# Audio attention: averages in four 32-column tiles of one bank, half of the keys turned by TensorE

## The reference

```python
a = _layer_norm(audio_kv, ln_gamma, ln_beta)              # 8 batches x 1500 tokens x 256
Q = (hidden_states @ Wq.T)...                             # 8 batches x 56 queries, 16 heads of 16
K = (a @ Wk.T)...
V = (a @ Wv.T)...
scores = einsum('bhtd,bhsd->bhts', Q, K) * scale
scores = where(mask, scores, -inf)
attn = softmax(scores, axis=-1)
out = einsum('bhts,bhsd->bhtd', attn, V)
out = out.transpose(0, 2, 1, 3).reshape(B, Tt, D) @ Wo.T
return hidden_states + tanh(gate) * out
```

## Time and profile before

| | us |
|---|---|
| median of 3 runs | 1460.28 |
| lowest, highest | 1457.51, 1460.68 |
| the profiled execution | 1458.31 |
| its span in the profile | 1456.5 |
| in it, from DVE's first audio minimum to the end | 323.7 |

### The profile page before, as it was taken

One profiled execution on the slowest core, in us unless ns is written; L12 is line 12 of the kernel. 1 busy time (PEld: TensorE's weight loads), 2 busy tenths in 40 slices (PEclk: granted clock), 3 DMA queues, 4 the chain that ended last, 5 costly groups with the idle time before them and its releaser, 6 DMA issues.

```text
span 1456.5 us, 24705 instructions
## 1 busy us (share of the span) xinstructions
PE 1409.2 (97%) x9188; PEld 889.1 (61%) x9188; DVE 983.2 (68%) x2028; ACT 869.1 (60%) x1566; POOL 486.1 (33%) x393
## 2 busy tenths in 40 slices
PE   9999999999999999999999999999899999999987
PEld 5466666666666654566666666666554455555545
DVE  6856555555555658776566566565558998889886
ACT  6654554455455547645544544554445798889986
POOL 5546334334334200234523523530001433333300
PEclk9999999999999999999999999999999999999999
DMA  6399889889988831599988989887622799999998
GB/s 212 98 224 185 177 175 182 176 171 180 180 170 178 163 99 29 145 195 186 182 168 179 182 169 180 182 166 149 179 55 55 150 221 213 217 210 214 223 201 159
DMA packets 671059, 246.88 MB, mean 170 GB/s; under 512 B 643693, under 2 KB 645213, under 8 KB 670941
## 3 DMA queue, kind: packets, MB, share of 16 engines
q1 hardware_dynamic: 670940, 245.32, 83.1%
HBM read 85.28 MB, written 0.52 MB: 59 GB/s over the span
## 4 chain that ended last, share of the span: by engine, by line
PE 73%; DVE 8%; DMA 7%; ACT 6%; SPq 3%; issue 3%; ACTq 0%; DVEq 0%
PE SC L790 39%; PE PV L790 34%; DMA core<-qc 3%; DVE qc L1588 2%; ACT qc L1321 2%; DVE prob L1570 2%; DMA core<-core 1%; ACT prob L1312 1%; DVE core L1629 1%; ACT core L1305 1%; DMA qc<-core 1%; SPq L519 1%; DMA core<-in_wv_dram 1%; SPq L561 1%; ACT small L1329 1%
## 5 line engine op out<-in xcount | busy, mean ns | idle before, releaser
L790 PE MATMUL PV<-core 128*128 128x256 f16 (+1 forms) x4800 | 540.0, 270 | 16.1 <-DMA core<-core 6.1
L790 PEld LDWEIGHTS PV<-core 128*128 128x128 f16 x4800 | 458.9, 98 | 85.6 <-issue 13.9
L1253 ACT ACTIVATE prob<-SC,core 128x500 f32<-128x500 f32 x336 | 223.9, 674 | 413.9 <-DVE core L1594 413.9
L1563 DVE TENSOR_REDUCE mx<-SC 128x1 f32<-128x500 f32 x336 | 224.9, 670 | 327.5 <-PE SC L790 327.5
L790 PE MATMUL SC<-ctxT,qc 128*128 128x500 f16 x2016 | 443.7, 374 | 0.0
L790 PEld LDWEIGHTS SC<-ctxT,qc 128*128 128x128 f16 x2016 | 196.2, 97 | 206.5
L718 POOL CAST ctxT<-stage 128x750 f16<-128x750 f32 x64 | 69.1, 1079 | 438.6 <-PE SC L790 240.8
L1621 DVE SCALAR_TENSOR_TENSOR core<-prob,core 128x1500 f16<-128x1500 f32 x112 | 194.7, 1738 | 3.8 <-ACT core L1262 3.7
L1262 ACT ACTIVATE core<-prob 128x1500 f16<-128x1500 f32 x112 | 162.9, 1455 | 3.5
L790 PE MATMUL SC<-ctxT 128*128 128x512 f16 x552 | 132.0, 382 | 4.3 <-DVE core L1629 4.1
L790 PE MATMUL SC<-qc 128*128 128x512 f16 x480 | 114.8, 384 | 12.8 <-DVE mx L1570 12.8
(11 more groups left out here) (143 smaller groups left out, 1329.4 us busy)
## 6 DMA issues: line engine op xcount, KB each, us to landing
stage<-in_ctx_nat_dram SPq DMA_DIRECT2D x64, 384.0 KB, 3.9
stage<-in_ctx_t_dram SPq DMA_DIRECT2D x64, 375.0 KB, 3.4
stage<-in_ctx_p_dram SPq DMA_DIRECT2D x32, 384.0 KB, 3.9
core<-in_wq_dram SPq DMA_DIRECT2D x8, 512.0 KB, 3.6
core<-in_wk_dram SPq DMA_DIRECT2D x8, 512.0 KB, 3.6
core<-in_wv_dram SPq DMA_DIRECT2D x8, 512.0 KB, 5.5
core<-in_wo_dram SPq DMA_DIRECT2D x8, 512.0 KB, 5.1
core<-core SPq DMA_TRANSPOSE x224, 4.0
```

The source lines that it names most:

```text
L790: return nc.tensor.matmul(o, a, c, start=start, stop=stop, skip_group_check=skip)
L1253: nc.scalar.activation(prob[:, i, c * CW:c * CW + w], SETS[i][c][:, 0:w], ACT.Exp, bias=nmax[:, i, :], accum_out=sum3[:, i, c:c + 1]).then ...
L1563: nc.vector.tensor_reduce(mx3[:, t % 2, c:c + 1], SETS[t % 2][c][:, 0:w], AX_X, ALU.max)\
```

## The change

1. **Averages.** A window was 24 matmuls, each with 128 weights columns (four heads) and 224 moving columns (four heads x 56 queries); only the four 32 x 56 blocks on the diagonal were used. Now each head is a matmul of its own, with 32 weight columns and 56 moving columns into its own 32 partitions: 96 matmuls, and the output is 128 x 56. They all go to bank `PV[0]`, except in the last batch, where windows alternate between both banks as before.
2. **Their copy.** `pick_average` is one activation of 128 x 56 instead of four of 32 x 56. With one bank, a window's first matmul now waits until the copy of the window just before it is done (`attn_ready` n, where it was n-1).
3. **Keys.** Of the four pieces of a batch (1 to 7), pieces 1 and 3 (units 3, 4, 5, 9, 10, 11) are no longer transposed by DMA. At the head of slots 1 to 6, ahead of the scores, PE multiplies one such unit with a float16 identity (`turn_unit`: 4 matmuls of 128 columns into `PV[1]`), and ACT copies it to `kst` (`turned_keys`, 128 x 512, between the window copy and the exponential). `turn_unit` waits for the unit's low half (`m_lo`) and for ACT's copy of the turn before. Slots 1 to 6 turn units 3, 4, 5, 9, 10, 11 in this order.
4. **Moves.** DMA transposes of keys stay in slots 0 and 4 (pieces 0 and 2); the mask's load moves from slot 1 to 0 and its first activation from slot 3 to 2. The float16 identity is a DVE copy in the MLP (f = 4), in the first half of `dmean`, which is not used after that.

```diff
+        SLOT_KEYS = {0: 0, 4: 2}
-        SLOT_KEYS = {0: 0, 2: 1, 4: 2, 5: 3}
+        TENSOR_PIECES = (1, 3)
+        SLOT_TURN = {1: 3, 2: 4, 3: 5, 4: 9, 5: 10, 6: 11}
+        TURNS = len(SLOT_TURN)
...
+        def average_bank(b, w):
+            return PV[w % 2 if b == B - 1 else 0]
...
-                if s == 1 and b + 1 < B:
+                if s == 0 and b + 1 < B:
                     mask_load(b + 1)
...
+            def turn_unit(n):
+                if turns_through(n) == 1:
+                    pe.wait_ge(ident_ready, 1)
+                    pe.wait_ge(aq_lo, NW)
+                else:
+                    pe.wait_ge(kp_full, turns_through(n) - 1)
+                pe.wait_ge(m_lo, n + 1)
+                for w in range(NW):
+                    ins = mm(PV[1][:, w * P:(w + 1) * P], core16[:, key_slot(n) + w * P:key_slot(n) + (w + 1) * P],
+                             ident16, True, True)
+                ins.then_inc(kp_mm, 1)
...
-                if n >= 2:
-                    pe.wait_ge(attn_ready, n - 1)
+                if n >= 1:
+                    pe.wait_ge(attn_ready, n - 1 if b == B - 1 and w > 0 else n)
...
-                        ins = mm(PV[w % 2][:, 0:WR], values(NT * b + j, w)[0:r, :],
-                                 probT[0:r, i * NT + j, w * WR:(w + 1) * WR], j == 0 and i == 0, j == NT - 1 and i == 1)
+                        v = values(NT * b + j, w)
+                        for h in range(HW):
+                            own = slice(2 * KA * h, 2 * KA * (h + 1))
+                            c = w * WR + h * Q
+                            ins = mm(average_bank(b, w)[own, 0:Q], v[0:r, own], probT[0:r, i * NT + j, c:c + Q],
+                                     j == 0 and i == 0, j == NT - 1 and i == 1)
...
                 for y in range(RT * B + 3):
+                    if turned_unit(y) is not None:
+                        turn_unit(turned_unit(y))
                     if y < RT * B:
                         audio_scores(y)
...
+            def turned_keys(n):
+                b, j = divmod(n, NT)
+                act.wait_ge(kp_mm, turns_through(n))
+                if b >= 2:
+                    act.wait_ge(as_score, RT * (b - 1))
+                nc.scalar.activation(kst[:, b % 2, j, :, :].rearrange("p w t -> p (w t)"), PV[1][:, :],
+                                     ACT.Copy).then_inc(kp_full, 1)
...
-                for h in range(HW):
-                    own = slice(2 * KA * h, 2 * KA * (h + 1))
-                    ins = nc.scalar.activation(attnT[own, w, b * Q:(b + 1) * Q], PV[w % 2][own, h * Q:(h + 1) * Q],
-                                               ACT.Identity, scale=1.0 / PROB_SCALE, bias=vbias[own, w:w + 1])
-                ins.then_inc(attn_ready, 1)
+                nc.scalar.activation(attnT[:, w, b * Q:(b + 1) * Q], average_bank(b, w)[:, 0:Q], ACT.Identity,
+                                     scale=1.0 / PROB_SCALE, bias=vbias[:, w:w + 1]).then_inc(attn_ready, 1)
...
-                    if s == 3 and b + 1 < B:
+                    if s == 2 and b + 1 < B:
                         mask_row(b + 1, (b + 1) % 2)
```

More of the change, by code:

```diff
@@ L186, in build @@
         dmean = sb("dmean", [P, P])
+        ident16 = dmean[:, 0:P // 2].bitcast(F16)
         one = sb("one", [P, 1], F16)
@@ L242, in build @@
         ta_hi = sem("ta_hi")
-        kt_full = [sem(f"kt_full{k}") for k in range(2)]
+        kt_full = [sem(f"kt_full{k}") for k in range(PIECES)]
+        kp_mm = sem("kp_mm")
+        kp_full = sem("kp_full")
+        ident_ready = sem("ident_ready")
         pad_ready = sem("pad_ready")
@@ L399, in slot_units, with turned_unit, turns_through, by_tensor @@
             return [NT * (b + 1) + j for j in SLOT_UNITS[s] if 0 <= y and NT * (b + 1) + j < NT * B]
+        def turned_unit(y):
+            b, s = divmod(y, RT)
+            return NT * (b + 1) + SLOT_TURN[s] if s in SLOT_TURN and b + 1 < B else None
+        def turns_through(n):
+            b, j = divmod(n, NT)
+            return TURNS * (b - 1) + 1 + list(SLOT_TURN.values()).index(j)
+        def by_tensor(n):
+            return n >= NT and n % NT // JP in TENSOR_PIECES
         def at_slot(table, y):
@@ L415, in unit_bank, with key_slot @@
             return (TB + [M])[n % NB]
+        def key_slot(n):
+            return (VSLOTS + n % KSLOTS) * UNIT
         def unit_out(n, half):
@@ L549, in turn_keys @@
                 o = kst[:, b % 2, k * JP:(k + 1) * JP, :, :].rearrange("p j w t -> p (j w) t")
-                sp.dma_start_transpose(o, core16[:, at:at + JP * UNIT]).then_inc(kt_full[g % 2], 16)
+                sp.dma_start_transpose(o, core16[:, at:at + JP * UNIT]).then_inc(kt_full[k], 16)
             def turn_audio(y):
@@ L1004, in audio_scores @@
                         for k in range(c, c + 2):
-                            pe.wait_ge(kt_full[k % 2], 16 * (PIECES // 2 * b + k // 2 + 1))
+                            if b > 0 and k in TENSOR_PIECES:
+                                pe.wait_ge(kp_full, turns_through(NT * b + JP * (k + 1) - 1))
+                            else:
+                                pe.wait_ge(kt_full[k], 16 * (b + 1))
                     o = SC[:, at:at + 512].rearrange("p (j t) -> p j t", t=P)
@@ L1019, in audio_average @@
                 y = RT * b + FIRST_TILE[w]
-                if n >= 2:
-                    pe.wait_ge(attn_ready, n - 1)
+                if n >= 1:
+                    pe.wait_ge(attn_ready, n - 1 if b == B - 1 and w > 0 else n)
+                if w == 1 and b == B - 1:
+                    pe.wait_ge(kp_full, TURNS * (B - 1))
                 if w == 0:
@@ L1300, in unit_high @@
                 act.wait_ge(m_mm, n + 1)
-                if n % JP == 0 and g >= 2:
-                    act.wait_ge(kt_full[g % 2], 16 * (g // 2))
+                if n >= KSLOTS and by_tensor(n - KSLOTS):
+                    act.wait_ge(kp_mm, turns_through(n - KSLOTS))
+                elif n >= KSLOTS and n % JP == 0:
+                    b, k = divmod(g - 2, PIECES)
+                    act.wait_ge(kt_full[k], 16 * (b + 1))
                 if n >= VSLOTS:
@@ L1354, in audio_attention @@
                         pick_average(*at_slot(SLOT_PICKS, y))
+                    if turned_unit(y) is not None:
+                        turned_keys(turned_unit(y))
                     if b < B:
@@ L1776, in _ @@
                     mask_term_of(0)
+                if f == 4:
+                    nc.vector.tensor_copy(ident16, ident[:, :]).then_inc(ident_ready, 1)
                 if f == 5:
```

## The result

| | before | after |
|---|---|---|
| median of 4 runs, us | 1460.1 (1457.5 to 1460.7) | 1496.8 (1489.7 to 1506.2) |
| profiled execution, us | 1458.3 | 1490.4 |
| its span, us | 1456.5 | 1488.6 |

The changed kernel is slower: the ratio is 1.026, 95% interval [1.022, 1.030]. The forecast was 1490, 1470 to 1512. The runs lie in pairs, 1489.7 and 1490.4 at a mean granted clock of 0.99, 1503.1 and 1506.2 at 0.98.

The account below looks back on a forecast made before the run. No single engine bounds it, but the hand-over between PE and DVE. Waits 32.8, swallowed -2.8, one bank 3.9, last batch and end -4.3, DMAs -1, clock 3: 31.6 onto 1458.3, so 1490 us, range 1470 to 1512.

Parts of the forecast that it names:

- unit 3's wait: Slot 1: turn waits for the unit's low half, delaying scores and DVE; +1.5 us, six times, 9.0; -2.8 for waits swallowed.
- unit 9's wait: Slot 4: turn waits for DVE's last work of slot 3, delaying the scores; +1.9 us, seven times, 13.3.
- unit 10's wait: Slot 5: turn waits for the unit's low half, delaying the scores; +1.5 us, seven times, 10.5.
- one bank, batches 1 to 6: Slots 1 and 2: second window waits for the first's copy, delaying slot 3's scores; +0.65 us, six times, 3.9.
- relief by fewer DMAs, less PE: Two of eighteen transposes a batch go, shortening DMA waits: 1 us saved in all (0 to 3).
- clock, batches 0 to 6: PE may fall to half rate behind slot 4's 2.9 us idle time; 0 to 11 us in all, 3 taken.
- last batch and end: Shorter copies save 2.8 us in three last-batch slots; half a window and a copy at the end save 1.5: -4.3.
- Rival 1: The DMA queue is the bound and the change relieves it: faster, 1443 us; 11%.
- rival 4: The clock falls in most batches: 1497 to 1505 us, counted within the forecast's 75%.
- The window: Averages as 96 narrow matmuls: 1.2 us a window, between 0.6 and 3.5, against 2.31 before.
- rivals 3: Averages' tiles don't run side by side: 3.5 us a window instead of 1.2, about 1525 us; 8%.
- Rival 5: A window as long as before, 2.3 us: about 1507 us, within the forecast; 10 of its hundredths.

Follow-up runs that it names:

- run 1: Changed kernel with each unit's turn placed behind the scores of its slot on PE instead of ahead: 1446.0 us, ratio 0.993 to the kernel before.
- run 5: Changed kernel with only piece 1 turned by PE, piece 3 transposed by DMA in slot 5, turns still ahead of the scores: 1460.9 us, ratio 1.002.
- run 6: Run 1's kernel with only unit 9's turn put back ahead of the scores of slot 4: 1465.4 us, ratio 1.005 to the kernel before.
- run 2: Kernel before with only the narrow averages and their single copy; two banks, all keys by DMA, mask where it was: 1467.0 us, ratio 1.007.
- run 3: Run 2's kernel with the transposes of key pieces 1 and 3 left out in batches 1 to 7, nothing in their place: 1442.4 us, ratio 0.989.
- run 4: Run 1's kernel with averages as 24 wide matmuls and four copies again, all in one bank: 1471.5 us, ratio 1.009 to the kernel before.
- run 8: Changed kernel with extra overwritten matmuls filling PE's idle time before the turns of units 3, 9 and 10: 1484.7 us, ratio 1.019.

## Why the prediction was right

Its mechanism was the right one: the turn's wait, passed on through the scores to DVE. The sum came so near partly by luck, since some of its smaller terms were off in opposite directions. For the profiled executions (forecast 31.6, measured 32.1 us):

| term | forecast | measured | from |
|---|---|---|---|
| unit 3's wait, less what it swallows of before's own waits | 9.0 - 2.8 | 6.5 | slots 0 to 1, less 1.7 of clock |
| unit 9's wait | 13.3 | 13.8 | slots 3 to 4, less 2.9 of clock |
| unit 10's wait | 10.5 | 9.6 | slots 4 to 5 |
| one bank, batches 1 to 6 | 3.9 | 2.0 | slots 2 to 3 |
| relief by fewer DMAs, less PE | -1 | -5.6 | slots 5 to 6 and 6 to 0; 5.1 of it in batch 3 |
| clock, batches 0 to 6 | 3 | 4.6 | below |
| last batch and end | -4.3 | +3.0 | below |
| before the stage | 0 | -1.9 | first minimum |

**The waits: right, each by itself.** +1.5, +1.9 and +1.5 us were read off as the unit's end less the scores' old start, less DVE's lead. Batch 5 gave +1.58, +1.94 and +1.37. Run 1 shows that it is the order and nothing else in the change, run 5 that each wait goes with its unit, run 6 the 1.94 alone. The turn's copy took 0.59 us for the 0.68 taken, so that ACT's busy time in batch 5 fell by 0.4 us where it was to rise by 0.4.

**The relief: sized too small.** In the profiled run after it shows only where no turn waits. The last two intervals of batch 3 took 6.98 and 8.94 us before and take 4.80 and 6.03 now, which is 5.1 of the 5.6 us. The clock also fell there before, so how much of this is relief of the queue is open. The relief's full size shows without the stalls. The DMAs had been put at 1 us; run 2 against run 3 makes two transposes a batch worth 24.5 once the averages are fast, the clock behind the waits included. The step that failed was to price a transfer by the waits for it in the trace of before. There PE was busy 37.8 us of a batch and waited 4.6 us over the stage for these transposes; in run 2, with PE busy some 4 us less a batch, it was 31.0.

**Rival 1**, 1443 us by relief, was turned down because PE could never reach the turns late; that held. But its figure is nearly what lay under the stalls: run 1, 1446. In its parts it is less near. Its 11 us of batches came (batches 0 to 6 of run 1 are 11.6 us shorter than before), its 4.3 us of the last batch and the end did not (1.2 longer), and 2.3 came ahead of the stage.

**The last batch and the end: wrong sign.** This is the term of the sum that failed: -4.3 forecast, +3.0 measured. The copies and half windows did get shorter, and from slot 3 to 4 the last batch takes 3.70 us for 4.86. Two things outweighed that. The first is the one bank. The prediction counted its cost in six batches, but slots 1 and 2 of the last batch still make two windows of batch 6, both in `PV[0]`. PE waits 2.28 us for the copy between them, and the twelve scores behind take 3.77 us for 2.75, partly at the lower clock:

```profile
1452.06 1.31 PE L819 MATMUL PV<-core 128*32 128x56 f16 x96 [2.28 <-ACT small L1392]
1453.31 3.77 PE L819 MATMUL SC<-qc 128*128 128x512 f16 x12
```

That makes the interval from slot 2 to 3 6.97 us for 4.90. Runs 2 and 3, which have two banks, took 4.65 us there, and every run with one bank 5.7 or more (run 1: 7.02).

The second is the end. Its lines in the kernel before (the last sums) and after:

```profile
1451.85 2.14 PE L790 MATMUL SC<-small,ctxT 128*128 128x56 f32 x16
```

```profile
1480.81 0.75 PE L819 MATMUL PV<-core 128*32 128x56 f16 x48 [2.84 <-DMA core<-qc]
1481.99 0.75 PE L819 MATMUL PV<-core 128*32 128x56 f16 x48 [0.43 <-DMA core<-qc]
1482.67 3.66 PE L819 MATMUL SC<-small,ctxT 128*128 128x56 f32 x16
...
1486.01 0.63 DVE L1775 SCALAR_TENSOR_TENSOR xT<-SC,tg,xT 128x56 f32<-128x56 f32 x2 [8.60 <-PE SC L819]
```

Against the earlier trace rows the half window is shorter (0.75 for 1.31), as forecast, and so is its copy (0.31 for 1.24). But the last half window starts 1.6 us later, counted from DVE's last low half (1474.56, before 1444.91), because the transposes land later. Then the sixteen sums take 3.66 us for 2.14, at a granted clock of 0.50 in that stretch, where it was 1.00 before. PE had stood idle 2.84 us shortly before. Runs 1 to 3, all with the narrow averages, have 3.66 or 3.67 us for these sums, run 4 with the wide ones 2.13.

**The clock: right in the profiled run, too small for the median.** Three falls in it: 9.04 for 7.35, 8.58 for 7.11, and in batch 0 9.37 for the 7.90 of run 8. Two of the four executions have a lower mean clock and stand 13 and 16 us higher, so the median of 1496.8 is midway. These two were about the prediction's rival 4, 1497 to 1505, which it had put inside the forecast; one stands a microsecond beyond it.

**The window: 1.02 us for the 1.2 taken; rivals 3 and 5 are out.** Ninety-six matmuls of 56 columns start 11 ns apart. They stream as many columns in all as the 24 wide ones (5376), so one after another at the wide ones' pace they would take the same 2.31 us; they took 1.02, so the column tiles do work side by side, though not four times as fast. Rival 5 is the case of the Trainium skill's rule ("TensorEngine Tiling (Array Packing)", Instruction Overhead) that a matmul of one column takes as long as one of 60, so that a dimension that is small already shouldn't be divided. Read as a price for these 96 matmuls, the rule disagrees with this trace.

**One bank**: the window waits 1.09 us for ACT's copy, and the interval of batch 5 grew by 0.37 (forecast 0.65), since the window (1.02 us for 1.2) and the turn (0.22 for 0.3) were shorter than taken. With the 2.1 us of the last batch it cost 4.1 in all, near the 3.9 of the sum, but that is chance: six batches cost less than forecast, and the seventh was forgotten.

**Two slips in the working** change little. The lower end of 1474 adds up to 1476 (stalls of 24 for 33, no clock loss, 3 us by DMA), and 2.3 us isn't midway between the window's bounds of 0.6 and 3.5, whose middle is 2.05.

What is open: what decides whether the clock falls behind an idle time of 2.6 us (it did and didn't in the same slot of the same execution, run 6), and how run 4's loss divides between full engines and the one bank.

## What to carry to other kernels

Place an instruction that may wait behind, not ahead of, the work that others wait for: on an in-order engine its wait is theirs, and the price can be read beforehand as the awaited result's end, less the old start of what stands behind, less the lead. Where PE, a queue and DVE all run near their limits, an edit that relieves one can lose (run 2) until a second relieves the next, so test the parts apart and together, with their waits put right first. Idle time made on PE can cost more than itself, because the clock may fall behind it: in run 6 that was 5.8 us beside 13.6 of waiting.

## What the runs showed of the hardware

Three idle times of 2.2 to 2.8 us on PE in every batch cost some 10 us of clock over seven batches (changed kernel against run 8, an estimate across two chips); the executions of the changed kernel lie between 0.98 and 0.99 of mean granted clock. Filling only the gap of slot 4 made the falls behind the others regular (1498 us); filling all three removed them (1485). Ninety-six float16 matmuls of 56 columns over four column tiles started 11 ns apart. And a DMA share near 1.15 stood for a batch of 36.5 us as for one of 42.2: whether it is the limit was told by the waits for its transposes, not by the share.
